# A four-stage convolution kernel: tiles of the selective scan alternate in time direction, scans write over their decays, and the layer norm's two VectorE steps move to GpSimd and ScalarE

## The reference

```python
xn = (xf - mu) / jnp.sqrt(var + EPS) * ln_g + ln_b            # layer norm over 64 channels
chunks = xn.reshape(B, L, 4, C // 4)...                       # 4 chunks of 16 channels, L = 3136 steps in time
xz = jnp.einsum('gld,ed->gle', x, in_proj_w); xi, z = jnp.split(xz, 2, axis=-1)
u = silu(causal_conv4(xi) + conv_b)
dt, Bm, Cm = jnp.split(jnp.einsum('gld,ed->gle', u, x_proj_w), [1, 17], axis=-1)
delta = softplus(dt * dt_proj_w + dt_proj_b); A = -exp(A_log)
def step(h, inputs):                                          # for 32 inner channels x 16 states
    dA = jnp.exp(d_t[..., None] * A)
    h = h * dA + (d_t * u_t)[..., None] * B_t[:, None, :]
    y = jnp.einsum('gdn,gn->gd', h, C_t)
y = (ys + u * D) * silu(z)
out = chunks + jnp.einsum('gld,ed->gle', y, out_proj_w)
```

## Time and profile before

| | us |
|---|---|
| median of 3 runs (9377.71 to 9384.65) | 9379.95 |
| the profiled execution, its own time | 9385.57 |
| its span | 9383.8 |
| VectorE busy in the span | 6973.6 |
| GpSimd busy | 5475.1 |
| ScalarE busy | 5322.5 |
| TensorE matmuls busy | 7771.6 |

### The profile page before, as it was taken

The page is one execution under the profiler, slowest core; times in us unless marked ns, Lnnn a source line. Parts: engine busy times, 40 slices in busy tenths (PEclk is TensorE's granted clock), DMA queues, the critical chain, the costliest instruction groups (busy, mean ns, idle before and its releaser), DMA issues. The chain is left out here.

```text
span 9383.8 us, 134613 instructions
## 1 busy us (share of the span) xinstructions
PE 7771.6 (83%) x30601; PEld 4082.9 (44%) x30601; DVE 6973.6 (74%) x9361; ACT 5322.5 (57%) x9326; POOL 5475.1 (58%) x4944
## 2 busy tenths in 40 slices
PE   9977777787777778777777777777778999999996
PEld 9962222222222222222222222222225899959996
DVE  7759999999999999999999999999991122212222
ACT  0237777777777777777777777777770133201432
POOL 0008888888888888888898888888880000000000
PEclk9988888888888888788887888888889999999998
DMA  9646565655655656555665565656651000030002
GB/s 175 168 122 167 159 166 162 165 163 162 166 163 165 163 162 166 163 164 164 164 167 162 163 164 165 166 161 166 163 162 56 17 0 0 18 86 0 0 0 55
DMA packets 1108342, 1202.02 MB, mean 128 GB/s; under 512 B 460432, under 2 KB 1094800, under 8 KB 1107344
## 3 DMA queue, kind: packets, MB, share of 16 engines
q1 hardware_dynamic: 871568, 1117.24, 44.2%
q10 hardware_dynamic: 236032, 77.08, 3.6%
HBM read 961.04 MB, written 155.41 MB: 119 GB/s over the span
## 5 line engine op out<-in xcount | busy, mean ns | idle before, releaser
L644 POOL TENSOR_TENSOR prod<-hs,bsp 128x448 f32<-128x448 f32 x3584 | 4067.8, 1158 | 647.1 <-PE ps L655 464.1
L632 DVE TENSOR_TENSOR_SCAN hs<-da,hs,ps 128x448 f32<-128x448 f32 x3072 | 3490.8, 1136 | 0.0
L623 DVE TENSOR_TENSOR ps<-ps,bsp 128x448 f32<-128x448 f32 x3585 | 2186.6, 610 | 249.1 <-PE ps L607 223.0
L607 PE MATMUL ps<-stack,seld 96*128 96x448 bf16 x3587 | 1422.2, 411 | 1054.8 <-DVE hs L632 1001.9
L613 ACT ACTIVATE da<-da,nega 128x448 f32<-128x448 f32 x3588 | 2235.9, 661 | 16.0 <-issue 7.2
L906 PE MATMUL ps<-pv,ws 128*128 128x224 f32 x8800 | 1692.3, 354 | 9.4 <-ACT pv L1064 7.0
L906 PEld LDWEIGHTS ps<-pv,ws 128*128 128x128 f32 x8800 | 1657.3, 189 | 45.0 <-issue 7.7
L655 PE MATMUL ps<-prod,wc 128*32 128x448 f32 x7200 | 1551.4, 719 | 90.3 <-POOL prod L644 86.7
L607 PEld LDWEIGHTS ps<-stack,seld 96*128 96x128 bf16 x3587 | 347.8, 99 | 2660.5 <-DVE hs L632 2338.2
L1237 DVE SCALAR_TENSOR_TENSOR pv<-ps,R 128x224 f32<-128x224 f32 x880 | 422.4, 480 | 1279.0 <-PE ps L906 1279.0
L407 PE MATMUL ps<-xn,wtap 128*128 128x448 f32 x1808 | 982.3, 650 | 3.5 <-ACT bsp L467 3.5
(11 more groups left out here) (118 smaller groups left out, 7223.8 us busy)
## 6 DMA issues: line engine op xcount, KB each, us to landing
da<-delta_copy SPq DMA_DIRECT2D x3595, 224.0 KB, 3.6
stack<-parts SPq DMA_DIRECT2D x2700, 28.0 KB, 2.3
delta_copy<-dlt SPq DMA_DIRECT2D x225, 224.0 KB, 1.9
lnx<-in_x SPq DMA_DIRECT2D x118, 224.0 KB, 3.7
lny<-y_nchw SPq DMA_DIRECT2D x118, 224.0 KB, 4.3
x_column_pairs<-otile SPq DMA_DIRECT2D x225, 116.0 KB, 2.7
xpad<-x_column_pairs SPq DMA_DIRECT2D x32, 812.0 KB, 4.3
xpad<-in_x SPq DMA_DIRECT2D x64, 392.0 KB, 6.8
```

Of the source, the lines that this page charges most:

```text
L607: pe.matmul(ps[:, DU_BANK + j % 4, 0:T], seld[0:96, b, :], stack[:, st.t % 2, grp, :], start=True, stop=True).then_inc(S["du_spread"], 1)
L623: v.tensor_tensor(du, du, bsp[:, st.t % 2, 0, :], ALU.mult).then_inc(S["dbu_done"], 1)
L632: v.tensor_tensor_scan(hs[:, j, :], da[:, j % SLOTS, :], ps[:, DU_BANK + j % 4, 0:T], 0.0 if first else hs[:, j, T - 1:T], ALU.mult, ALU.add)\
L644: g.tensor_tensor(prod[:, j % 8, :], hs[:, j, :], bsp[:, st.t % 2, 1, :], ALU.mult)\
```

## The change

It has three parts. **Direction:** in every second tile (odd t) time runs backwards along the columns: `tap` and `z` read `xn` reversed, and all that follows of the tile is in that order until `project_out` reads `yg` backwards. **Scan in place:** `hs` is gone, `da` has one column more (T + 1) per unit, and the scan writes the states over the decays. The last state of a tile stands in the column next to those that the next tile's decays fill, and that tile scans 449 columns, with an immediate start of 1.0 and a drive of 0 in the first (columns 0 and T + 1 of the PSUM banks, zeroed once); before, it read its start from a column. So a unit's slot is free for its next load only when `times_c` has read it (`prod_done`), not when it is scanned. **Layer norm:** `ln_sum` is a ScalarE activation (`ln_affine`, task `scale_y`) and a GpSimd addition (`add_x`), `ln_scale` a GpSimd multiplication (`times_rstd`), and the gain goes into `ln_shift`'s activation. The tables move `relu`, `shift`, `rest1`, `delta`, and the parts' DMAs.

```diff
-ACT_AT = {2: ["relu", "cast0"], 4: ["cast1"], 5: ["silu", "u", "z", "exp"], 6: ["evacuate"], 7: ["lnc"], 8: ["bc0"],
-          9: ["dt"], 10: ["dt2", "bc1"], 11: ["lnv"], 13: ["clamp"], 14: ["shift"]}
-DVE_AT = {0: ["add_x"], 3: ["gate"], 11: ["scale"]}
-POOL_AT = {1: ["rest0"], 4: ["rest1"], 9: ["over"], 12: ["delta"], 13: ["delta_u"]}
-SP_AT = {1: ["copy"], 7: ["part0"], 10: ["part1"], 12: ["part2"], 13: ["store"]}
+ACT_AT = {0: ["scale_y"], 2: ["cast0"], 3: ["relu"], 4: ["cast1"], 5: ["silu", "u", "z", "exp"], 6: ["evacuate"],
+          7: ["lnc"], 8: ["bc0"], 9: ["dt"], 10: ["dt2", "bc1"], 11: ["lnv"], 13: ["clamp"], 15: ["shift"]}
+DVE_AT = {3: ["gate"]}
+POOL_AT = {1: ["rest0", "add_x"], 5: ["rest1"], 9: ["over"], 11: ["delta"], 13: ["delta_u", "times_rstd"]}
+SP_AT = {1: ["copy"], 5: ["part0"], 7: ["part1"], 9: ["part2"], 12: ["store"]}
...
-            da = sb(m, "da", [P, SLOTS, T])
-            hs = sb(m, "hs", [P, UN, T])
+            da = sb(m, "da", [P, UN, T + 1])
...
+        def span(buf, a, n, back):
+            return buf[:, a + n - 1:a - 1 if a else None:-1] if back else buf[:, a:a + n]
...
+        def ln_affine(a, st):
+            a.wait_ge(S["ln_loaded"], (st.ln + 1) * 32)
+            a.activation(lny[:, :], lny[:, :], ACT.Identity, bias=col(SHIFT2), scale=col(SCALE2)).then_inc(S["y_scaled"], 1)
+
+        def ln_sum(g, st):
+            g.wait_ge(S["y_scaled"], st.ln + 1)
+            g.tensor_tensor(lnx[:, :], lnx[:, :], lny[:, :], ALU.add).then_inc(S["x_summed"], 1)
...
+        def ln_scale(g, st):
+            g.wait_ge(S["rstd"], st.ln + 1)
+            g.tensor_tensor(xcen[:, :], xcen[:, :], xrstd[:, :], ALU.mult).then_inc(S["scaled"], 1)
...
-                sp.wait_ge(S["scan_done"], (st.tile - 1) * UN + (j + 9))
+                sp.wait_ge(S["prod_done"], st.tile * UN + (j + 1))
...
-            v.wait_ge(S["prod_done"], n + 1)
-            first = st.t % KT == 0
-            v.tensor_tensor_scan(hs[:, j, :], da[:, j % SLOTS, :], ps[:, DU_BANK + j % 4, 0:T],
-                                 0.0 if first else hs[:, j, T - 1:T], ALU.mult, ALU.add)\
-                .then_inc(S["scan_done"], 1)
+            h, bank = da[:, j, :], j % 4
+            if st.t == 0:
+                a, d, start = h[:, 1:T + 1], drives(bank), 0.0
+            elif st.t == KT:
+                a, d, start = h[:, T - 1::-1], drives(bank, 1, T + 1)[:, ::-1], 0.0
+            elif st.t % 2:
+                a, d, start = h[:, ::-1], drives(bank, 1, T + 2)[:, ::-1], 1.0
+            else:
+                a, d, start = h, drives(bank, 0, T + 1), 1.0
+            v.tensor_tensor_scan(a, a, d, start, ALU.mult, ALU.add).then_inc(S["scan_done"], 1)
```

More of the change, by code:

```diff
@@ L192, in build @@
             "y_summed", "y_gated", "out_mm", "out_evac", "out_stored0", "out_stored1")}
-        spread_in = [sem(f"c_spread_in{i}") for i in range(SLOTS)]
+        spread_in = [sem(f"c_spread_in{i}") for i in range(16)]
         D = {n: sem("d_" + n) for n in (
@@ L333, in build, with elements, drives @@
         DU_BANK, TMP_BANK, Y_BANK, O_BANK = 0, 5, 7, 7
+        def span(buf, a, n, back):
+            return buf[:, a + n - 1:a - 1 if a else None:-1] if back else buf[:, a:a + n]
+        def elements(j, t):
+            lo = 0 if t % 2 else 1
+            return da[:, j, lo:lo + T]
+        def drives(bank, lo=1, hi=T + 1):
+            return ps[:, DU_BANK + bank, lo:hi]
         class Step:
@@ L497, in ln_relu @@
                 a.wait_ge(S["centred"], st.ln)
[L498 to L505, removed]
+            a.activation(xres[:, :], lnx[:, :], ACT.Relu).then_inc(S["x_relu"], 1)
+        def ln_scale(g, st):
+            g.wait_ge(S["rstd"], st.ln + 1)
+            g.tensor_tensor(xcen[:, :], xcen[:, :], xrstd[:, :], ALU.mult).then_inc(S["scaled"], 1)
         def ln_shift(a, st):
@@ L606, in spread_du @@
             pe.wait_ge(S["scan_done"], st.tile * UN + j + 5)
-            pe.matmul(ps[:, DU_BANK + j % 4, 0:T], seld[0:96, b, :], stack[:, st.t % 2, grp, :],
+            pe.matmul(drives(j % 4), seld[0:96, b, :], stack[:, st.t % 2, grp, :],
                       start=True, stop=True).then_inc(S["du_spread"], 1)
         def decay(a, st, j):
-            a.wait_ge(spread_in[j % SLOTS], st.tile * (UN // SLOTS * 16) + (j // SLOTS + 1) * 16)
-            a.activation(da[:, j % SLOTS, :], da[:, j % SLOTS, :], ACT.Exp, scale=nega[:, j:j + 1])\
+            a.wait_ge(spread_in[j], st.tile * 16 + 16)
+            a.activation(elements(j, st.t), elements(j, st.t), ACT.Exp, scale=nega[:, j:j + 1])\
                 .then_inc(S["exp_done"], 1)
@@ L671, in project_out @@
                 o = ps[lo:lo + C, O_BANK, 0:T // 2]
-                pe.matmul(o, wcs("proj_out", 0, C), yg[:, odd:T:2], start=True, stop=False)
+                y = yg[:, T - 1 - odd:None if odd else 0:-2] if back else yg[:, odd:T:2]
+                pe.matmul(o, wcs("proj_out", 0, C), y, start=True, stop=False)
                 mm = pe.matmul(o, wcs("residual", s, C), xn[:, 3 + k * T + odd:3 + k * T + T:2], start=False, stop=True)
@@ L846, in _ @@
                             if name == "project":
-                                project_out(pe, tile, s, k)
+                                project_out(pe, tile, s, k, par == 1)
                             elif name == "last3":
@@ L1010, in _ @@
                                 evacuate(a, tile, par, before)
+                            elif name == "scale_y":
+                                if st.has_ln:
+                                    ln_affine(a, st)
                             elif name == "relu":
@@ L1117, in _ @@
                 v.sem_inc(S[f"out_stored{par}"], 16)
-            for k in range(6):
-                st = Ahead(k)
-                ln_sum(v, st)
-                ln_scale(v, st)
             for j in range(LEAD["drive"]):
@@ L1131, in _ @@
                         for name in DVE_AT.get(j, ()):
-                            if name == "gate":
-                                gate(v, tile, ub)
-                            elif name == "add_x":
-                                if st.has_ln:
-                                    ln_sum(v, st)
-                            elif st.has_ln:
-                                ln_scale(v, st)
+                            gate(v, tile, ub)
             tile, ub, s, k, par, before, img = ended(PAIRS, 0)
@@ L1254, in _ @@
             g.wait_ge(S["ready"], 4)
+            for k in range(6):
+                st = Ahead(k)
+                ln_sum(g, st)
+                ln_scale(g, st)
             st = Ahead(0)
@@ L1275, in _ @@
                                 delta_times_u(g, st)
-                            else:
+                            elif name.startswith("rest"):
                                 rest_of(g, st, int(name[4]))
+                            elif st.has_ln:
+                                if name == "add_x":
+                                    ln_sum(g, st)
+                                else:
+                                    ln_scale(g, st)
             barrier(g, 3)
```

40 lines of the change are left out of this document (18 added, 22 removed).

## The result

The changed kernel takes 9490.71 us (median of 4 runs, 9483.72 to 9497.23); the kernel before took 9381.99 in the same rounds. The ratio is 1.0113, with an interval of 1.0099 to 1.0128: slower, by 109 us, where 300 were forecast.

What follows compares the result with a forecast made beforehand. Plain tiles were taken as bound by a ScalarE-GpSimd loop, not VectorE. 112 norm tiles gave +291, 112 plain tiles 0, the start +9: +300, so 9680 us against the median 9380; range 9480 to 9830.

Steps and rivals of the forecast that it cites:

- R + 3.35: Norm tile: `cast1` starts 3.35 us after mark R (`rest0`) instead of 1.07, as `relu` waits for `add_x`.
- 2.3 us of delay: Norm tile: everything behind `cast1`, to `xsq`, `dt`, `sum0` and product 8, shifts by 2.3 us.
- C: Rival: VectorE is the bound, so scan and norm savings of 506 us make the kernel faster, 8875; 10%.
- D: Rival: backwards reads cost extra in odd tiles, +237 us, 9917 at most; 8%.
- in such a row one costs 1.09: GpSimd's instructions done in a row, products among them, cost 1.09 us each.
- Nothing again: Plain tiles: the new order on GpSimd changes no time, since `over` to `rest0` holds the same twelve instructions.
- +2.6 per norm tile: Norm tiles go from 29.8 to 32.4 us; over 112 tiles +291 us.
- R to P: Norm tile, from `rest0` to product 8's start: 13.56 us plus 2.3 makes 15.9.
- rival A: TensorE stays at full clock: `rest0` to product 8 is 14.2 us, a norm tile 30.7, the kernel 9490; 17%.
- P to R: Norm tile, from product 8 to the next `rest0`: 16.98 us becomes 16.5, with 15 GpSimd instructions instead of 14.
- I let the other waits vanish: Norm tile, product 8 to next `rest0`: the remaining waits, beyond scans 11 and 12 coming earlier, counted as none.
- Covered, by 0.7 us: Norm tile: `cast0`, queued behind `shift` on ScalarE, ends 0.7 us before `rest0` needs it.

Runs made afterwards that it cites:

- pitch_452: The changed kernel with units of `da` 452 columns apart instead of 449: 9619.39 us, ratio 1.0252.
- norm_part: The kernel before with only the layer norm part and its new tables, `hs`, direction and scans as before: 9626.04 us, ratio 1.0260.
- before_offset_2: The kernel before with only `hs` moved, its units beginning two words later: 9206.98 us, ratio 0.9816.
- scans_part: The kernel before with only direction, scan in place and loads waiting for products; layer norm and tables as before: 9295.95 us, ratio 0.9911.
- offset_2_relu_fill: The changed kernel with states at the fast place, `relu` behind `cast1`, two unused matmuls each ahead of `lnc` and `dt`: 9212.14 us, ratio 0.9823.
- scans_offset_2_fill: scans_offset_2 with three unused matmuls ahead of `dt` in the norm tiles: 9167.80 us, ratio 0.9775.
- scans_offset_2: The kernel before with direction and scan in place, layer norm left on VectorE, all states at the fast place: 9171.74 us, ratio 0.9777.
- offset_2: The changed kernel with units of `da` 452 columns apart and states 2 or 3 words past a multiple of four: 9382.76 us, ratio 1.0001.

## Why the prediction was right in sign and wrong in size

**Right: the mechanism of the norm tile.** `relu` behind `add_x` holds up `cast1` and all behind it. Forecast R + 3.35 for `cast1`, measured 3.20; forecast 2.3 us of delay, 2.12 at `dt` as a mean over all norm tiles. Moving `relu` behind `cast1` gave 75 us back, and the layer norm's move alone cost 244 (9626 against 9382). On top of that, pitch_452 shows the scans to be worth 7 us.

**Right: plain tiles are not bound by VectorE, and backwards reads are free.** With dear products, plain tiles take 26.52 with the shorter scans (pitch_452) and 26.54 with the long ones (norm_part), 26.60 before. 449 columns take 1078 ns on average in tiles of either direction. Rivals C and D are false; C's bound does appear once the products are fast, as before_offset_2 and scans_part show.

**The step that failed: "in such a row one costs 1.09", kept for the products after the change, and with it "Nothing again" for plain tiles.** A product's duration is no constant of the engine and the size. In the changed kernel the products average 1056 ns and not 1134, and that is worth 129 us (9619 against 9491). In the profiled executions it is 123: 71 in the plain tiles (0.63 x 112) and 53 in the norm tiles (0.48 x 111). The diff showed it: the pitch went from 448 to 449 elements. I counted that column as length and did not ask what it does to where operands begin.

**The term +2.6 per norm tile was too large even with dear products.** pitch_452 has 31.97 where 32.4 was forecast. Three things in it:
- *R to P.* I added 2.3 to 13.56, the value of one tile at a low clock, and set the sum against 29.8, a mean over tiles at both clocks; that tile itself took 30.54. Against its own kind the increment was 32.4 - 30.54 = 1.86, or +208 in place of +291. The true mean of R to P was 13.09 (the earlier trace rows show a tile of either clock).
- *The clock.* I had the longer idle time all fall ahead of `dt`. It went ahead of `lnc` instead, since `relu` was late for that too, and by `dt` the clock was often high again: in 66 of 111 norm tiles the clock was full from `dt` on and R to P is 14.1, rival A's 14.2, in the others 15.4 to 16.6. The mean is 14.81 (14.85 with dear products), so of the 2.12 us of delay 0.40 came back between `dt` and P. Rival A was half true. Its time, 9490, agrees with the result by accident: without the effect of the place the kernel takes 9619.
- *P to R* went the other way: 17.12 in pitch_452 for 16.5. "I let the other waits vanish" was wrong: `clamp` (0.68 us above) and `cast0` are waited for, 27.3 and 38.3 us in pitch_452, or 0.6 per norm tile, which is nearly the whole difference. What did vanish is the slowing of GpSimd's products beside VectorE's layer norm steps. And "Covered, by 0.7 us", said of `cast0` behind `shift`, held in every tile but the 15 where the loop begins again.

**The account.** Forecast +300, measured +111.6 in the profiled executions. Against the forecast, plain tiles are 79 lower (71 of it the place), norm tiles 107 (53 of it the place, 54 the first two errors less the third), the start 3.5 and the stretch behind the first R 0.8, and the end is 1.8 higher: together -189, but for rounding.

**A rule weighed again.** The layer norm's move cost 244 us alone, and still lost 44 with everything around it mended (offset_2_relu_fill against scans_offset_2_fill). The Trainium skill, GPSIMD Engine Reference, section Engine selection, wants such instructions on VectorE. The times agree, though what they show is the chain of waits and not the 1.6 in duration. And the last 44 us are no proof of the rule: the 47.8 us that `rest0` waits at the turns of the loop are as much, and no run is without them while the layer norm is off VectorE.

What stays open: what in the engine or memory makes the place matter; why TensorE's clock falls ahead of `dt` in some tiles and behind it in others; and what holds ScalarE at the turns of the loop, and with it whether the whole change with a `shift` placed otherwise would beat scans_offset_2.

## What to carry to other kernels

When a change alters a buffer's pitch or offset, read the duration of every instruction on that buffer again before costing anything: here two words of offset gave 1.8%, more than the whole change cost. Set an increment that is worked out on one tile against that tile, not against a mean over tiles of other kinds. And ask of a delay which engine's idle time it moves, and to ahead of which instruction. Look at the turns of a loop apart from its other passes: a wait there is small in the mean and, here, 43 us in the sum.

## What the runs showed of the hardware

- **A GpSimd product of two f32 operands depends on where they begin.** Count the word of four, from the start of its buffer, at which a state begins. 128x448: median 1134 ns at word 0 (before), 1132 at words 0 and 1 (pitch_452), 981 at word 2 (before_offset_2), 982 at words 2 and 3 (offset_2). In the changed kernel the states begin at all four words, with medians of 1133, 1131, 978 and 978, and the mean, 1056, is midway. The Trainium skill, SBUF — State Buffer, section "Door 1: The DMA port swizzle", says that memory has lines of 16 bytes and that crossing to a new one costs. Four words of f32 are such a line, which agrees with the period seen; that crossings at different moments are what helps is a guess that no run tests.
- **A GpSimd product is slowed beside some VectorE instructions.** In the kernel before, 212 of the 373 products that overlapped a layer norm step on VectorE (a SCALAR_TENSOR_TENSOR on 128x448 f32) took over 1.2 us, 1.53 on average; the other 3211 took 1.17 at most. In norm_part, without these steps on VectorE, the longest took 1.18.
- **A scan can run backwards and in place at no cost:** 1078 ns for 449 columns in tiles of either direction, 1076 for 448, and 1136 where it began from a column.
- **TensorE's granted clock fell behind gaps of a few us, and unused matmuls in the gap kept it high.** Before, `dt` took 1.83 us for two matmuls behind a gap of 2.58 us, at a granted clock of 0.50 (1.2 GHz), and 0.99 behind one of 1.75 us, at 1.00 (2.4 GHz); with three unused matmuls ahead of it each took 542 ns on average.
- **ScalarE stood still for 2.4 to 3.5 us at each of 15 turns of a hardware loop** in norm_part, behind an activation that had waited, with no wait that the profile shows. The kernel before, with another order there, has it in 2 turns of 15 (1.1 and 1.8 us).
